# Combine weights by transfers through memory in place of eight products, denominators by products of 32 rows

## What is computed

```python
h = layernorm(x) * (1 + ca) + sa                      # per row of the batch
q, k, v = split(h @ W_in.T)                           # 16 heads of 16 channels
num = (Tq * cumsum(Tk * v) * beta).sum(orders)
den = (Tq.sum(channels) * cumsum(Tk.sum(channels)) * beta).sum(orders)
x = x + ga * ((num / (den + 1e-7)) @ W_out.T)
h = layernorm(x) * (1 + cb) + sb
activation = sqrt(softplus(h @ routing_W.T + expert_bias))
top_vals, top_idx = top_k(activation, 2)
combine = sum(one_hot(top_idx, 8) * top_vals)         # 8 weights a token
routed = sum over e of combine[:, e] * (silu(h @ rW1[e] + rb1[e]) @ rW2[e] + rb2[e])
x = x + gb * (silu(h @ sW1 + sb1) @ sW2 + sb2 + routed)
```

## Time and profile before

| | before |
|---|---|
| median of 3 runs | 1034.9 us (1034.83 to 1036.24) |
| profiled execution | 1032.3 us, span of its instructions 1030.6 us |
| mean granted TensorE clock | 0.959 of full speed |
| busy: PE, DVE, ACT, POOL | 941.8, 849.2, 437.4, 398.4 us |
| transfers | 68.23 MB, mean 66 GB/s |

### The profile page before, as it was taken

The page is one execution under the profiler, slowest core; times in us unless marked ns, Lnnn a source line. Parts: engine busy times, 40 slices in busy tenths (PEclk is TensorE's granted clock), DMA queues, the critical chain, the costliest instruction groups (busy, mean ns, idle before and its releaser), DMA issues.

```text
span 1030.6 us, 14429 instructions
## 1 busy us (share of the span) xinstructions
PE 941.8 (91%) x4505; PEld 672.6 (65%) x4505; DVE 849.2 (82%) x1320; ACT 437.4 (42%) x637; POOL 398.4 (39%) x631
## 2 busy tenths in 40 slices
PE   3863659999999999999999999999999999989995
PEld 3643437676767676676767676776767676757773
DVE  2487898899999999899999899998989999896321
ACT  4343335353535445453536354454535363431320
POOL 2023453352625254443626153544535262434110
PEclk9876769999999999999999999999999999999998
DMA  7103131332414123323324142233332241414011
GB/s 284 47 10 74 44 80 52 66 80 49 106 31 105 30 65 83 70 61 64 91 43 102 25 97 53 62 72 73 72 63 61 43 91 23 102 22 91 18 21 21
DMA packets 45052, 68.23 MB, mean 66 GB/s; under 512 B 4595, under 2 KB 33726, under 8 KB 44998
## 3 DMA queue, kind: packets, MB, share of 16 engines
q0 software_dynamic: 15360, 33.56, 19.1%
q1 hardware_dynamic: 28066, 31.63, 9.0%
q10 hardware_dynamic: 1572, 2.45, 0.7%
HBM read 25.14 MB, written 17.32 MB: 41 GB/s over the span
## 4 chain that ended last, share of the span: by engine, by line
PE 56%; DVE 17%; issue 5%; DVEq 1%; DMA 1%; POOLq 0%; ACT 0%; SPq 0%
PE ring L1246 21%; PE acc L1369 15%; PE tr L1299 7%; PE tr L1321 5%; DVE feat L943 3%; DVE hid L1091 3%; PE cfb L1347 3%; PE tr L1237 2%; DVE prod L978 2%; DVE feat L968 2%; DVE feat L897 1%; PE misc L1272 1%; DVE stats L368 1%; PE acc L1356 1%; DVE feat L964 1%
## 5 line engine op out<-in xcount | busy, mean ns | idle before, releaser
L1369 PE MATMUL acc<-w,hid 128*128 128x256 f32 x1152 | 285.2, 392 | 1.1 <-DVE hid L1091 1.1
L1369 PEld LDWEIGHTS acc<-w,hid 128*128 128x128 f32 x1152 | 207.7, 190 | 56.2 <-issue 29.0
L637 POOL DMA_DIRECT2D feat<-feat x48 | 46.2, 963 | 356.0 <-DVE feat L968 158.2
L795 ACT ACTIVATE hid<-ring,b1row 128x512 f32<-128x512 f32 x144 | 98.3, 683 | 184.7 <-PE ring L1246 184.6
L1091 DVE TENSOR_TENSOR hid<-hid,cfb 128x512 f32<-128x512 f32 x128 | 86.7, 677 | 73.9 <-PE cfb L1347 73.6
L750 ACT ACTIVATE feat<-ring,bqkv 128x512 f32<-128x512 f32 x96 | 66.1, 689 | 127.9 <-PE ring L1246 127.9
L943 DVE TENSOR_TENSOR_SCAN feat<-zero,carry,feat 128x512 f32<-128x512 f32 x80 | 112.0, 1450 | 0.0
L943 DVE TENSOR_TENSOR_SCAN feat<-zero,feat 128x512 f32<-128x512 f32 x80 | 105.4, 1367 | 0.0
L1246 PE MATMUL ring<-n2H,w1H 128*128 128x512 f32 x288 | 101.9, 435 | 0.0
L1246 PE MATMUL ring<-n2H,w1L 128*128 128x512 f32 x288 | 91.0, 397 | 0.0
L1246 PE MATMUL ring<-n2L,w1H 128*128 128x512 f32 x288 | 90.7, 396 | 0.0
(11 more groups left out here) (155 smaller groups left out, 1608.5 us busy)
## 6 DMA issues: line engine op xcount, KB each, us to landing
feat<-feat POOLq DMA_DIRECT2D x48, 512.0 KB, 4.6
xin<-in_L_attn_x SPq DMA_DIRECT2D x16, 512.0 KB, 5.7
feat<-inv_rows SPq DMA_DIRECT2D x32, 256.0 KB
out<-x SPq DMA_DIRECT2D x16, 512.0 KB, 5.0
out<-fin POOLq DMA_DIRECT2D x16, 512.0 KB, 6.2
gates<-gate_rows SPq DMA_DIRECT2D x16, 128.0 KB, 5.1
feat<-in_L_wmod SPq DMA_DIRECT2D x1, 1536.0 KB, 13.2
w<-in_L_ffn_rW ACTq DMA_DIRECT2D x1, 1024.0 KB, 10.1
```

Source lines behind the costliest of these rows:

```text
L637: g.dma_start(f(into), f(of), accum_op=ALU.add).then_inc(added[n], 16)
L795: a.activation(hid[:, e % NG], ring[bank][:, :], ACT.Silu, bias=b1row[:, e:e + 1]).then_inc(ring_copied, 1)
L1369: last = mm(acc[t // 2][:, t % 2], hid[:, e % NG, t * P:(t + 1) * P], w2[:, e], start=False, stop=(e == E), skip_group_check=True)
```

## The change

1. The eight spreading products go, with `cfsel`, `cfB` and their 512 KB of constants. VectorE writes the combine weights into columns 50 to 57 of the tile `split`, so that the transposes that are there anyway bring them into rows 50 to 57. ScalarE copies rows 32 to 57 in full precision to `cfT`. SP writes 8 rows of it to memory (`cf_rows`), waits, and reads them back onto 128 partitions: row 1 alone (256 KB), rows 2 to 6 in one transfer (1.25 MB), rows 7 and 8 (512 KB) after the first two experts have been weighed, since `cfw` has six slots. `weigh_hidden` reads `cfw` from SBUF.
2. The denominators: for each block of 128 tokens two products with 32 weight columns, written to 32 of the 128 rows. There are again eight products of 64 columns. The inverse is written to memory in the matching order, 8 by 16 rows. The constants shrink by 960 columns more, so that the load of constants is 199 KB in place of 674.5 and 512 KB.

```diff
@@ spread_inverse, and new behind it
-                sp.dma_start(inv_rows.rearrange("h (b t) -> (h b) t", b=NB), denom[:, 1]).then_inc(inv_written, 16)
+                sp.dma_start(inv_rows.rearrange("h (b t) -> b h t", b=NB), denom[:, 1]).then_inc(inv_written, 16)
...
+            def spread_weights(i, p):
+
+                c = number(i, p)
+                sp.wait_ge(cf_ready, 2 * c + 1)
+                ge(sp, cf_spread[2], 16 * c)
+                sp.dma_start(cf_rows, cfT[SPL:SPL + E, :]).then_inc(cf_written, 16)
+                ge(sp, hidw_ready, E * c)
+                sp.wait_ge(cf_written, 16 * (c + 1))
+                for n, (a, b) in enumerate(((0, 1), (1, NW))):
+                    sp.dma_start(cfw[:, a:b], cf_rows[a:b].partition_broadcast(P)).then_inc(cf_spread[n], 16)
+
+            def spread_last_weights(i, p):
+
+                c = number(i, p)
+                sp.wait_ge(hidw_ready, E * c + E - NW)
+                sp.dma_start(cfw[:, 0:E - NW], cf_rows[NW:E].partition_broadcast(P)).then_inc(cf_spread[2], 16)
@@ step of SP
                     spread_inverse(i, p)
+                if number(i, p) and number(i, p) <= CB * B:
+                    spread_weights(*later(i, p, -1))
+                if loads or i < B:
                     store_x1(i, p)
                 if loads:
                     load(sp, i + 2, p)
+                if number(i, p) and number(i, p) <= CB * B:
+                    spread_last_weights(*later(i, p, -1))
@@ combine_rows on ScalarE
-                a.activation(cfB[:, :], misc[0:SPL // 2, :], ACT.Copy).then_inc(cf_ready, 1)
+                ge(act, cf_written, 16 * c)
+                a.activation(cfT[QS:SPL + E, :], misc[QS:SPL + E, :], ACT.Copy).then_inc(cf_ready, 1)
@@ weigh_hidden on VectorE
-                dve.wait_ge(cfb_ready, E * c + e)
-                v.tensor_tensor(hid[:, e % NG], hid[:, e % NG], cfb[:, :], ALU.mult).then_inc(hidw_ready, 1)
+                dve.wait_ge(cf_spread[0 if e == 1 else 1 if e <= NW else 2], 16 * (c + 1))
+                v.tensor_tensor(hid[:, e % NG], hid[:, e % NG], cfw[:, (e - 1) % NW], ALU.mult).then_inc(hidw_ready, 1)
@@ denominators
-                for b in range(NB):
-                    last = mm(misc[:, 0:TB], cv["densum"][:, b * P:(b + 1) * P],
-                              prod[:, b * TB:(b + 1) * TB], start=(b == 0), stop=(b == NB - 1))
+                for b in range(2):
+                    for t in range(NT):
+                        at = t * P + b * TB
+                        last = mm(misc[t * QS:(t + 1) * QS, 0:TB], cv["densum"][:, b * QS:(b + 1) * QS],
+                                  prod[:, at:at + TB], start=(b == 0), stop=(b == 1))
@@ products that spread, and their call in expert_down
-            def spread_weights(i, p, e):
-
-                mm(cfb[:, :], cfsel[:, e - 1], cfB[:, :], start=True, stop=True).then_inc(cfb_ready, 1)
...
-                if e < E:
-                    spread_weights(i, p, e + 1)
```

More of the change, by code:

```diff
@@ L28 @@
 NB = P // H
+NW = 6
 TB = CT // NB
@@ L73, in constants @@
             w = GAMMA[n] if n in (0, 2, 4) else 1.0
-            for b in range(NB):
-                c["densum"][row, b * P + (half * HPH + h) * NB + b] = w
+            for b in range(2):
+                c["densum"][row, b * QS + b * H + half * HPH + h] = w
             c["kshift"][row, 0] = {1: -0.5 * DH, 3: -0.125 * DH}.get(n, 0.0)
@@ L81, in constants @@
     c["tie"][:] = np.where(j < e, 0.0, np.finfo(np.float32).tiny).astype(np.float32).ravel()
-    for x in range(E):
-        for part in range(3):
-            c["cfsel"][part * E + x, x * P:(x + 1) * P] = 1.0
     return np.concatenate([c[k] for k in CONSTS], axis=1)
@@ L102, in sem @@
             return ctx.enter_context(nc.semaphore(name))
-        const = sb("const", [P, sum(CONSTS.values()) - CONSTS["cfsel"]])
+        const = sb("const", [P, sum(CONSTS.values())])
         cv, at = {}, 0
         for k, n in CONSTS.items():
-            if k != "cfsel":
-                cv[k] = const[:, at:at + n]
-                at += n
+            cv[k] = const[:, at:at + n]
+            at += n
         ident = cv["ident"]
@@ L155, in build @@
         logT = sb("logT", [P, CT])
-        route = sb("route", [P, 5, NT, E])
-        L_, RANK, C0, C1, CF = range(5)
+        route = sb("route", [P, 4, NT, E])
+        L_, RANK, C0, C1 = range(4)
         top = sb("top", [P, NT, 8])
@@ L205, in build @@
         r2f, r2h, r2l = tmp_late(D), tmp_late(D), tmp_late(D)
-        assert at_late[0] <= NG * CT and NT * D == KD * HID * (E // 2) and E * P == NT * D
+        assert at_late[0] <= NG * CT and NT * D == KD * HID * (E // 2)
         tr = [ctx.enter_context(nc.psum_tensor(f"tr{k}", [P, CT], f32)) for k in range(2)]
@@ L253, in build @@
         split_T, cf_ready = sem("combine_transposed"), sem("combine_rows")
-        cfb_ready, hidw_ready = sem("combine_spread"), sem("hidden_weighted")
+        cf_written, cf_spread = sem("combine_written"), [sem(f"combine_spread{n}") for n in range(3)]
+        hidw_ready = sem("hidden_weighted")
         expert_done = sem("expert_done")
```

26 lines of the change are left out of this document (12 added, 14 removed).

## The result

The changed kernel takes 1018.6 us (median of four runs, 1017.0 to 1021.0) against 1035.2 us of the kernel before on the same chip, a ratio of 0.9846 with a 95% interval of 0.9826 to 0.9865: faster by 1.5%. The forecast was 1025, with a range of 998 to 1040 and faster as the likeliest sign. The sign and the range held, the sum was 6 us too high. That agreement says less than it seems to: two terms of each step were well off and partly cancelled, which the experiments show. That is luck, not a sum that was right.

What follows compares the result with a forecast made beforehand. The prediction took TensorE's products to set the pace, in a ring with VectorE; 1032.3 us - 9.4 (full steps) + 7.8 (clock) - 4.6 (last steps) - 2.5 (start) = 1023.6, plus 2.6 to the median: about 1025, range 998 to 1040.

Steps and rivals of the forecast that it cites:

- two terms of each step: Wait before expert 1 for row 1, 1.05 us odd, 1.5 even; VectorE's list, fixed but for 0.15 us more weighing.

## What to carry to other kernels

Before costing a shorter wait, look at what the neighbour engine does in that time: a wait can be the slot in which it works undisturbed, and whoever closes the wait pays for the overlap. Read a list's durations against the same operation elsewhere in the trace; two scans of 4.50 us beside two of 2.33 are 2 us that no sum of "busy" shows. And an engine that is busy for 99% of a step need not set it: take some work away and see whether the step follows. Last, a total of waits over a run says little before it is split by stage: 24 of 57 us here lay where their end gained almost nothing.

## What the hardware showed

*VectorE and GpSimd take turns.* In the rows above the later one of two overlapping operations that both read only SBUF ends as if it had begun when the earlier one ended: the scans that start at 613.32 beside a product that ends at 615.65 end 2.19 us after it; the product at 630.74 ends 1.09 us after GpSimd's end at 633.08; the weighing at 613.52 ends 0.55 after 615.73. GpSimd stands too when it is the later: its product takes 2.40 us alone, and 3.32 or 3.37 when one of VectorE's began just before. Operations of VectorE with an operand in PSUM or with only one operand were not stretched (1.29 and 1.40 us beside the product at 589.92). The Trainium skill says this of operations with two operands in SBUF ("SBUF — State Buffer", SBUF: two separate sides): an exclusive lock, the first to start keeps it for the whole instruction. These rows agree.

*Products with few columns.* The denominators are 16 passes of 64 columns before and after; with 32 weight columns in four column groups they take 0.36 us, with 128 they took 1.7, almost five times as long. I had expected about twice.

*Company on the queue.* 256 KB onto 128 partitions land in 3.1 us alone and in 4.7 with 1.25 MB issued 0.4 us behind them and two transfers of 512 KB behind that. A write of 16 KB takes 1.5 us to the issue that waits for it, and 3.5 to 4.0 in steps 3 to 14, where an accumulate of 512 KB has gone out some 2.5 us ahead of it.

*The clock after an idle time.* Behind idle times of TensorE of 2.07 to 2.33 us before expert 7 the granted clock fell to 0.50 in some steps, and behind 2.23 to 2.37 us at the same place it stayed at 1.00 in others. A fall cost 1.1 us, and eight products of 512 columns in the idle time prevented it.
